# Scan stage: the sum into the states as three products of split operands

## The chip, the cores and the metric

The kernel runs on one core of a Trainium2 chip. The metric is the device time of one execution in microseconds. Times of the kernel before are from three runs, and one more execution was recorded by the hardware profiler; rows below come from that one.

## The reference, cut to what matters

Two transformer-like layers over 2048 rows of 512 values: differential attention, a mixture of experts, a Mamba-2 scan, and a feed-forward block with int8 weights. The change lies in the scan. Per head (64 heads of 64 channels, state size 128), the reference computes

```python
x_dt = x * dt[..., None]
Y_diag = einsum('bclhn,bcshn,bhcls,bcshp->bclhp', C_c, B_c, Lmat, x_dt)
decay_states = exp(A_cum[..., -1:] - A_cum)
states = einsum('bclhn,bhcl,bclhp->bchpn', B_c, decay_states, x_dt)
new = prev * exp(d_k)[..., None, None] + s_k          # step by step
Y_off = einsum('bclhn,bchpn,bhcl->bclhp', C_c, prev_states, exp(A_cum))
g = (Y_diag + Y_off + D_param * x) * silu(z)          # then a row norm, then @ W_out.T
```

`states` is the sum into the states: B of a chunk times x, weighted by dt and by its decay to the end of the chunk.

## The kernel before, in words

The stages are `qkv`, `attention`, `attend_out`, `experts`, `scan` and `finish`, one after the other, each with its own five instruction streams, ordered by hand and tied by semaphores. An engine works its stream strictly in order, so whatever stands behind a waiting instruction waits too. The scan takes the span's stretch from about 1650 to 3175 us.

The scan does 128 steps (`STEPS`): 16 chunks of 128 rows times 8 groups of 8 heads (512 channels). Four steps make a batch (`t // QT`): four chunks of one group. The document calls the steps of a batch the first to the fourth (`t % QT` from 0 to 3). There are 32 batches, and 4 of them belong to group 0. While a batch is scanned, the 8 in-projection tiles of the next one are computed, 3, 2, 2 and 1 in its four steps (`SHARE`), and the convolutions of its four x tiles by VectorE, two in the first and two in the second step (`CONVOLVED`).

In step t the engines do this, in the order of their streams:

- TensorE: `turn_x(t+1)` (transposes of x), `outputs(t)` (fp32 products of 128 columns), `states(t)` (the sum into the states, one fp32 product of 512 columns), some in-projection tiles, `project_out(t-1)`, the other tiles.
- ScalarE: `decays(t+1)` (eight Relu, a table load, one Exp), then `gh` (the high part of the gated output, a Copy to fp32r) and its square, then reads of in-projection tiles and the Silu of convolved tiles (`x_silu`).
- VectorE: `weigh_x(t+1)` gives `xdt`, `weigh_c` gives `ce`, `gate(t)` gives `gx`, `next_state(t)`, `weigh_decays(t+1)` gives `M`, `rest(t)` gives `gl` (the low part), the convolutions, `add_out(t-1)`. In the first step both convolutions stand before `add_out`, in the second one before and one behind.
- GpSimd: `sd` (the decayed state), `decay_inputs(t+1)` gives `xdd` (x with its weights), and `ssq` (sum of squares; in group 0 ScalarE writes it and GpSimd has none).

A value "split" into two fp32r parts is a high part (a Copy to fp32r) and a low part (the rest, a subtraction); `product3` multiplies two split operands with three fp32r products. The in- and out-projection already work so.

The fourth step's `turn_x` needs all four `x_silu` of the next batch, and the last of them stands in the third step of ScalarE's stream, behind `gh` and its square (the list `late`).

Of the kernel before, what the change touches and what calls it, by code (L numbers as in the profile page):

```python
# [956 lines left out]
def experts(nc, g, X, xh, xl, lr, w, space, sources, chan_bc, dt_bias, A_log, mv, hist, x2, D):  # L957
# [25 lines left out]
    with ExitStack() as ctx:  # L983
# [9 lines left out]
        z, dA = carve([P, QT, NH]), carve([P, QT, NH])  # L993
        u, sq = (carve([P, QT * NH]) for n in range(2))
        s2 = sb("ex_s2", [P, QT * NH])
# [3 lines left out]
        rest, ea = carve([NH, CHUNK]), carve([NH, CHUNK])  # L999
        Bt, CB = g.later[:, :].rearrange("p (c n) -> p c n", n=P), g.masked[:, 1, :].rearrange("p (c n) -> p c n", n=P)  # L1000
        bias, eA, chan = sb("ex_bias", [P, NH]), sb("ex_eA", [P, NH]), sb("ex_chan", [P, 2, TAPS + 1])
# [16 lines left out]
        upto_sums, asum_made, ea_made, asum_turned = sem("upto_sums"), sem("asum_made"), sem("ea_made"), sem("asum_turned")  # L1018
        bt, bt_read, cb, cb_made = sem("bt"), sem("bt_read"), sem("cb"), sem("cb_made")
        x2_out, xT_out = sem("x2_out"), sem("xT_out")  # L1020
# [27 lines left out]
        with nc.Block() as block:  # L1048

            @block.sync  # L1050
            def _(sp):
# [13 lines left out]
                for s in range(3, SLOTS + 1):  # L1065
                    if 0 <= s - 3 < TT:
                        sp.wait_ge(normed, s - 2)
                        sp.dma_start(x2[cols(s - 3), :], X[:, s - 3, :]).then_inc(x2_out, 16)
                    i = s - 4
                    if 0 <= i < TT and i % QT == QT - 1:  # L1070
                        c = i // QT
                        sp.wait_ge(x_low, i + 1)
                        for n, part in enumerate((xh, xl)):
                            sp.dma_start(D["xT"][n][:, :, chunk(c)], part[:, :, chunk(c)].bitcast(F32)).then_inc(xT_out, 16)
                    c, part = at(s - 1)
                    if part == 2:
                        for made_by, name, src, out in ((asum_made, "acum", asum, asum_out), (ea_made, "expa", ea, ea_out)):
                            sp.wait_ge(made_by, c + 1)
                            for grp in range(GROUPS):
                                sp.dma_start(D[name][grp * TT + QT * c:grp * TT + QT * (c + 1), :].rearrange("c (h l) -> h c l", l=CL),  # L1080
                                             src[grp * GH:(grp + 1) * GH, :].rearrange("h (c l) -> h c l", l=CL)).then_inc(out, 16)
                    if part == 3:
                        sp.wait_ge(sm_copied, c + 1)
                        sp.wait_ge(sm_exped, 2 * c + 2)
                        sp.wait_ge(sm_turned, c + 1)
                        sp.dma_start(D["small"][:, :, QT * c:QT * (c + 1), :, :], sm[:, :, :, :, :]).then_inc(small_out, 16)
                        sp.wait_ge(bc_silu, c + 1)
                        sp.dma_start(D["C"][:, chunk(c)], acc[:, 1, :]).then_inc(c_out, 16)
                        sp.wait_ge(bt_read, c + 1)
                        sp.dma_start(D["B"][:, QT * c:QT * (c + 1), :], Bt).then_inc(b_out, 16)  # L1090
                        sp.wait_ge(cb_made, c + 1)
                        sp.dma_start(D["CB"][:, QT * c:QT * (c + 1), :], CB).then_inc(cb_out, 16)
                for out, count in ((x2_out, TT), (xT_out, 2 * NCH), (small_out, NCH), (ea_out, GROUPS * NCH), (asum_out, GROUPS * NCH),
                                   (c_out, NCH), (b_out, NCH), (cb_out, NCH)):
                    sp.wait_ge(out, 16 * count)
# [123 lines left out]
            def _(act):  # L1219
# [22 lines left out]
                def scan_part(c, part):  # L1242
# [33 lines left out]
                    if part == 3:  # L1276
                        act.wait_ge(bt, c + 1)
                        if c:
                            act.wait_ge(b_out, 16 * c)
                        act.activation(flat(Bt), bank(c, "bt")[:, :], ACT.Copy).then_inc(bt_read, 1)  # L1280

# [19 lines left out]
            def _(dve):  # L1301
# [66 lines left out]
                def scan_part(c, part):  # L1368
                    if part == 1:
# [3 lines left out]
                        else:  # L1373
# [62 lines left out]
def scan(nc, g, D, tables, hist, ssq_dram, acc_dram, w8, Wgate, Wup):  # L1436
# [26 lines left out]
    with ExitStack() as ctx:  # L1463
# [3 lines left out]
        acc, ssq = sb("sc_acc", [P, QT, E]), sb("sc_ssq", [P, GT, CHUNK])  # L1467
        Bt, Ct, CB = sb("sc_B", [P, QT, NS]), sb("sc_C", [P, CHUNK]), sb("sc_CB", [P, QT, P])
        chan, dtab = sb("sc_chan", [P, DI // P + 2, TAPS + 1]), sb("sc_dtab", [P, DI // P, 2])
# [37 lines left out]
        with nc.Block() as block:  # L1507

            @block.sync
            def _(sp):  # L1510
# [135 lines left out]
            def _(pe):  # L1646
# [74 lines left out]
            def _(act):  # L1721
# [39 lines left out]
                decays(0)  # L1761
                late = []
# [32 lines left out]
            def _(dve):  # L1795
# [483 lines left out]
def two_layers(nc, x, xT, Wq, Wk, Wv, Wo, lq1, lk1, lq2, lk2, first, gate, up, down, lora_b, scan_first, chan_table,  # L2279
# [5 lines left out]
    with ExitStack() as ctx:  # L2285
# [81 lines left out]
```

## Time and profile before

| | us |
|---|---|
| median of three runs | 3590.73 (3584.45 to 3592.86) |
| profiled execution, its own time | 3585.86 |
| its span | 3583.9 |
| TensorE busy over the span | 3375.8 (94%) |
| VectorE busy | 2675.5 (75%) |
| ScalarE busy | 2118.0 (59%) |
| GpSimd busy | 881.7 (25%) |
| `sc_ps` product (the sum into the states), both halves of 128 | 145.1 |
| `sc_xdd` on GpSimd, 128 | 245.9 |

Busy counts the time in which an engine had an instruction under way, a blocked one too. The shares are over the whole span; the scan's own stand in the rows below. The profiled execution is 4.87 us below the median of the three runs.

### The profile page before, as it was taken

How to read it: one execution, taken by the hardware profiler on the slowest of the kernel's cores; microseconds unless marked ns; L12 is line 12 of the kernel's file. 1: busy time of each engine (PE TensorE's matmuls, PEld its weight loads, DVE VectorE, ACT ScalarE, POOL GpSimd, SP SyncE). 2: the span in 40 equal slices, each digit the busy share in tenths (PEclk: the TensorE clock that was granted, in tenths of full speed). 3: DMA queues.
4: the chain of work that ended last, by engine and by line, in shares of the span. 5: the costliest groups of instructions: out<-in, count | busy, mean ns of one | idle time of the engine just before them, and what ended most of it. 6: DMA issues, size and time to landing. Idle time of an engine off the chain costs nothing. (4 is left out here: it accounts for less than half of the span.)

```text
span 3583.9 us, 58360 instructions
## 1 busy us (share of the span) xinstructions
PE 3375.8 (94%) x20672; PEld 2381.6 (66%) x20672; DVE 2675.5 (75%) x5242; ACT 2118.0 (59%) x3392; POOL 881.7 (25%) x818
## 2 busy tenths in 40 slices
PE   8889999999999888986999999999999999979998
PEld 6644444444444466764777777777777777758886
DVE  3577777777777284565999999989999899964444
ACT  3146666666666633443777777777777777753332
POOL 0022222222222210001344434344444344420000
PEclk9989999999999988997999999999999999989999
DMA  7443443443442311137666776677667766640100
GB/s 230 76 89 88 107 99 90 107 90 92 111 83 89 110 39 32 71 103 237 210 223 230 259 237 224 233 245 246 222 221 247 252 227 227 221 144 27 36 12 24
DMA packets 264128, 529.34 MB, mean 148 GB/s; under 512 B 32544, under 2 KB 55200, under 8 KB 260768
## 3 DMA queue, kind: packets, MB, share of 16 engines
q1 hardware_dynamic: 263840, 525.62, 47.2%
q8 instruction: 166, 2.72, 0.3%
q14 instruction: 122, 1.00, 0.1%
HBM read 429.55 MB, written 95.42 MB: 146 GB/s over the span
## 5 line engine op out<-in xcount | busy, mean ns | idle before, releaser
L510 ACT ACTIVATE probs<-prob_scores 128x1024 f32<-128x1024 f32 (+3 forms) x640 | 572.8, 897 | 380.7 <-PE prob_scores L440 372.1
L460 PE MATMUL times_v<-probs,VS 128*64 128x256 f32 (+2 forms) x4608 | 612.4, 382 | 14.1 <-ACT outT L537 13.0
L557 DVE TENSOR_REDUCE part_max<-ring 128x1 f32<-128x512 f32 x720 | 462.7, 685 | 115.5 <-PE ring L432 113.7
L49 PE MATMUL sc_pip<-sc_xh,sc_wl 128*128 128x512 f32 x1024 | 455.0, 444 | 25.0 <-DMA sc_xl<-x_low 18.3
L1618 POOL TENSOR_TENSOR sc_xdd<-sc_xdt,sc_small 128x512 f32<-128x512 f32 x128 | 245.9, 1921 | 844.4 <-DVE sc_xdt L1827 844.4
L460 PEld LDWEIGHTS times_v<-probs,VS 128*64 128x64 f32 x4608 | 279.7, 136 | 253.9 <-issue 162.8
L51 PE MATMUL sc_pip<-sc_xh,sc_wh 128*128 128x512 f32 x1024 | 405.1, 396 | 0.0
L50 PE MATMUL sc_pip<-sc_xl,sc_wh 128*128 128x512 f32 x1024 | 403.8, 394 | 0.0
L1752 ACT ACTIVATE sc_M<-sc_later,sc_small 128x128 f32<-128x128 f32 x1024 | 311.8, 389 | 0.0
L1818 DVE SCALAR_TENSOR_TENSOR sc_ca<-sc_xr,sc_chan,sc_ca 128x512 f32<-128x512 f32 x384 | 290.9, 757 | 13.6
L440 PE MATMUL prob_scores<-QS,KS 50*128 50x512 f32 (+3 forms) x1280 | 298.7, 463 | 1.4 <-ACT probs L510 1.4
L440 PEld LDWEIGHTS prob_scores<-QS,KS 50*128 50x128 f32 x1280 | 119.6, 184 | 214.1 <-ACT probs L510 120.8
L49 PEld LDWEIGHTS sc_pip<-sc_xh,sc_wl 128*128 128x128 f32 x1024 | 193.8, 189 | 100.8 <-issue 44.9
L554 DVE CUSTOM_DVE_ANT_0 masked_scores<-ring,later_keys 128x128 f32<-128x128 f32 x480 | 216.3, 488 | 52.6 <-PE ring L432 49.3
L432 PE MATMUL ring<-KS,QS 48*128 48x512 f32 (+3 forms) x1200 | 235.7, 388 | 12.8 <-DVE part_max L557 8.6
L50 PEld LDWEIGHTS sc_pip<-sc_xl,sc_wh 128*128 128x128 f32 x1024 | 194.1, 190 | 68.0 <-issue 29.2
L1636 POOL TENSOR_TENSOR sc_ssq<-sc_ssq,sc_sq 128x512 f32<-128x512 f32 x112 | 163.4, 1459 | 306.3 <-ACT sc_sq L1780 306.3
L51 PEld LDWEIGHTS sc_pip<-sc_xh,sc_wh 128*128 128x128 f32 x1024 | 193.5, 189 | 43.5
L1667 PE MATMUL sc_py<-sc_M,sc_xdt 128*64 128x128 f32 x2048 | 207.2, 281 | 10.4 <-DVE sc_M L1838 10.4
L368 POOL TENSOR_SCALAR_AFFINE_SELECT probs<-probs 128x256 f32<-128x256 f32 x256 | 104.6, 408 | 456.3 <-ACT probs L510 456.3
L1864 DVE TENSOR_TENSOR sc_gl<-sc_gx,sc_gh 128x512 fp32r<-128x512 f32 x128 | 216.3, 1690 | 0.1
L375 POOL TENSOR_TENSOR w_lo<-w_raw,w_hi 128x512 fp32r<-128x512 f32 x96 | 122.8, 1279 | 354.3 <-ACT w_hi L521 349.0
(328 smaller groups left out, 7179.2 us busy)
## 6 DMA issues: line engine op xcount, KB each, us to landing
sc_wh<-scan_W_high SPq DMA_DIRECT2D x256, 256.0 KB, 2.8
sc_wl<-scan_W_low SPq DMA_DIRECT2D x256, 256.0 KB, 3.5
sc_later<-scan_acum SPq DMA_DIRECT2D x128, 512.0 KB, 4.7
sc_ce<-scan_expa SPq DMA_DIRECT2D x128, 512.0 KB, 5.3
sc_woh<-scan_Wo_high SPq DMA_DIRECT2D x128, 256.0 KB, 4.1
sc_wol<-scan_Wo_low SPq DMA_DIRECT2D x128, 256.0 KB, 4.9
w_raw<-in_Wg SPq DMA_DIRECT2D x64, 256.0 KB, 2.8
scan_W_high<-w_hi SPq DMA_DIRECT2D x64, 256.0 KB, 2.0
```

The source lines that it names most:

```text
L49: pe.matmul(out, ll, rh, start=start, stop=False)
L50: pe.matmul(out, lh, rl, start=False, stop=False)
L51: return pe.matmul(out, lh, rh, start=False, stop=stop)
L432: pe.matmul(slot(place["max", q, t, s])[:, 0:w], QS[q % NQK][rows, i * P:(i + 1) * P], KS[q % NQK][rows, c * CHUNK:c * CHUNK + w], start=T ...
L440: mm = pe.matmul(pb[u % 2][:, s, 0:w], KS[b][rows, j * P:(j + 1) * P], QS[b][rows, (c + 1) * CHUNK - w:(c + 1) * CHUNK], start=True, stop= ...
L460: mm = pe.matmul(po[MV * s:MV * (s + 1), CHUNK - w + n * h:CHUNK - w + (n + 1) * h], VS[p % 2][:, j, :], PT[u % NPT][:, s, n * h:(n + 1) * ...
L510: act.activation(PT[u % NPT][:, :, 0:w], pb[u % 2][:, :, 0:w], ACT.Exp).then_inc(exped, 1)
L554: dve.tensor_tensor_reduce(out=masked_out[:, s, 0:w], in0=slot(n)[:, 0:w], in1=later[:, CHUNK - w:], scale=1.0, scalar=NEG, op0=ALU.add, o ...
L557: dve.tensor_reduce(to, slot(n)[:, 0:w], AX.X, ALU.max).then_inc(emptied, 1)
L1618: pool.tensor_tensor(xdd[t % 2][:, :, :], xdt[t % 2][:, :, :], bc(t, 1), ALU.mult).then_inc(xdd_made, 1)
L1752: act.activation(M[t % 2][:, h, :], later[t % 2][:, h, :], ACT.Relu, bias=small[b % 2][:, c, 3, h:h + 1], scale=-1.0).then_inc(relued, 1)
L1818: dve.scalar_tensor_tensor(out=to, in0=src, scalar=w, in1=to, op0=ALU.mult, op1=ALU.add).then_inc(conv if last else conv_step, 1)
```

## The change

The one fp32 product of `states(t)` becomes `product3` over split operands, B (`Bh`, `Bl`) and the weighted x (`xdh`, `xdl`). B is split once, in the stage `experts`: ScalarE writes the high part where it copied B before, VectorE subtracts the low part, both go to DRAM and the scan loads both. The weighted x is split in each step: GpSimd computes `xdd` as before, but into one buffer instead of two, ScalarE copies it to fp32r (`high_inputs`), GpSimd subtracts (`low_inputs`).

```diff
@@ experts
-        Bt, CB = g.later[:, :].rearrange("p (c n) -> p c n", n=P), ...
+        Bh, Bl = g.later[:, :].bitcast(F32R), usq[:, :].bitcast(F32R)
...
-                        act.activation(flat(Bt), bank(c, "bt")[:, :], ACT.Copy).then_inc(bt_read, 1)
+                        act.activation(Bh[:, :], bank(c, "bt")[:, :], ACT.Copy).then_inc(b_high, 1)
...
+                        dve.wait_ge(b_high, c + 1)
+                        dve.tensor_tensor(Bl[:, :], bank(c, "bt")[:, :], Bh[:, :].bitcast(F32), ALU.subtract).then_inc(bt_read, 1)
@@ scan, SyncE
-                    sp.dma_start(Bt[:, c, :], D["B"][:, at, :]).then_inc(bc_in[c], 16)
+                    for n, part in enumerate((Bh, Bl)):
+                        sp.dma_start(part[:, c, :].bitcast(F32), D["B"][n][:, at, :]).then_inc(bc_in[c], 16)
@@ scan, GpSimd
                 def decay_inputs(t):
                     pool.wait_ge(xdt_made, t + 1)
-                    if t >= 2:
-                        pool.wait_ge(s_prod, t - 1)
-                    pool.tensor_tensor(xdd[t % 2][:, :, :], xdt[t % 2][:, :, :], bc(t, 1), ALU.mult).then_inc(xdd_made, 1)
+                    if t:
+                        pool.wait_ge(xdd_low, t)
+                    pool.tensor_tensor(heads(xdd[:, :]), xdt[t % 2][:, :, :], bc(t, 1), ALU.mult).then_inc(xdd_made, 1)
+
+                def low_inputs(t):
+                    pool.wait_ge(xdd_high, t + 1)
+                    if t:
+                        pool.wait_ge(s_prod, t)
+                    pool.tensor_tensor(xdl[:, :], xdd[:, :], xdh[:, :].bitcast(F32), ALU.subtract).then_inc(xdd_low, 1)
...
                     if t + 1 < STEPS:
                         decay_inputs(t + 1)
+                    if t + 1 < STEPS:
+                        low_inputs(t + 1)
@@ scan, TensorE
                 def states(t):
-                    pe.wait_ge(xdd_made, t + 1)
-                    pe.wait_ge(bc_in[t % QT], 48 * (t // QT // GROUPS + 1))
-                    pe.matmul(p_s[:, :], Bt[:, t % QT, :], xdd[t % 2][:, :, :], start=True, stop=True).then_inc(s_prod, 1)
+                    pe.wait_ge(xdd_low, t + 1)
+                    pe.wait_ge(bc_in[t % QT], 64 * (t // QT // GROUPS + 1))
+                    if t:
+                        pe.wait_ge(s_next, t)
+                    product3(pe, p_s[:, :], (Bh[:, t % QT, :], Bl[:, t % QT, :]), (xdh[:, :], xdl[:, :])).then_inc(s_prod, 1)
@@ scan, ScalarE
+                def high_inputs(t):
+                    act.wait_ge(xdd_made, t + 1)
+                    if t:
+                        act.wait_ge(s_prod, t)
+                    act.activation(xdh[:, :], xdd[:, :], ACT.Copy).then_inc(xdd_high, 1)
...
                     if t + 1 < STEPS:
                         decays(t + 1)
+                        high_inputs(t + 1)
```

On GpSimd, in a step of the last group, before (`sc_sd` begins a step; the three small `sc_ssq` rows stand in that group alone):

```order
L1629 TENSOR_TENSOR sc_sd<-sc_state,sc_small 128x512
L1618 TENSOR_TENSOR sc_xdd<-sc_xdt,sc_small 128x512
L1636 TENSOR_TENSOR sc_ssq<-sc_ssq,sc_sq 128x4x128
L1643 TENSOR_TENSOR sc_ssq<-sc_ssq 128x128 x3
L1629 TENSOR_TENSOR sc_sd<-sc_state,sc_small 128x512
```

and of the change, the same place:

```order
L1648 TENSOR_TENSOR sc_sd<-sc_state,sc_small 128x512
L1630 TENSOR_TENSOR sc_xdd<-sc_xdt,sc_small 128x512
L1636 TENSOR_TENSOR sc_xdl<-sc_xdd,sc_xdh 128x512
L1657 TENSOR_TENSOR sc_ssq<-sc_ssq,sc_sq 128x4x128
L1664 TENSOR_TENSOR sc_ssq<-sc_ssq 128x128 x3
L1648 TENSOR_TENSOR sc_sd<-sc_state,sc_small 128x512
```

One more subtraction stands between `sc_xdd` and `sc_ssq`, so `sc_ssq` and the next step's `sc_sd` are behind it.

On ScalarE, in a second step, before (`sc_M` is the Relu and Exp of `decays`, `sc_pip` an in-projection tile):

```order
L1752 ACTIVATE sc_M<-sc_later,sc_small 128x128 x8
L1755 ACT_TABLE_LOAD
L1755 ACTIVATE sc_M<-sc_M 128x1024
L1772 ACTIVATE sc_gh<-sc_gx 128x512
L1780 ACTIVATE sc_sq<-sc_gx 128x512
L1729 ACTIVATE sc_xr<-sc_pip 128x512
```

and of the change:

```order
L1775 ACTIVATE sc_M<-sc_later,sc_small 128x128 x8
L1778 ACT_TABLE_LOAD
L1778 ACTIVATE sc_M<-sc_M 128x1024
L1788 ACTIVATE sc_xdh<-sc_xdd 128x512
L1803 ACTIVATE sc_gh<-sc_gx 128x512
L1811 ACTIVATE sc_sq<-sc_gx 128x512
L1752 ACTIVATE sc_xr<-sc_pip 128x512
```

The row `sc_xdh` is new and stands behind the Exp and ahead of `sc_gh`; no table load is added. The other rows are those of before.

## Rows read from the trace of the kernel before

**Rows 1.** Busy time by stretch: the scan, then one batch of four steps.

```profile
1686.00:3174.00 1488.00, 1476.31 (x9318) 1165.11 (x9317) 1370.18 (x2110) 1100.40 (x2009) 613.36 (x409) 1.00 0.69 231
...
2499.50:2546.30 46.80, 46.80 (x298) 37.08 (x296) 43.87 (x69) 35.09 (x65) 19.46 (x12) 1.00 0.67 228
```

**Rows 2.** Timeline of TensorE, start of a fourth step: start us, us, engine.

```profile
2521.98 0.40 PE L51 MATMUL sc_pip<-sc_xh,sc_wh 128*128 128x512 f32 x1
2522.21 0.60 PE L1653 MATMUL sc_pxt<-ident,sc_xT 128*128 128x128 f32 x4
...
2524.64 1.13 PE L1677 MATMUL sc_ps<-sc_xdd,sc_B 128*128 128x512 f32 x2
2525.20 0.79 PE L49 MATMUL sc_pip<-sc_xh,sc_wl 128*128 128x512 f32 x1
2525.83 0.39 PE L50 MATMUL sc_pip<-sc_xl,sc_wh 128*128 128x512 f32 x1
```

**Rows 3.** Timeline of GpSimd in a second step.

```profile
2500.44 1.95 POOL L1618 TENSOR_TENSOR sc_xdd<-sc_xdt,sc_small 128x512 f32<-128x512 f32 x1 [7.41 <-DVE sc_xdt L1827]
...
2505.89 1.29 POOL L1636 TENSOR_TENSOR sc_ssq<-sc_ssq,sc_sq 128x512 f32<-128x512 f32 x1 [3.50 <-ACT sc_sq L1780]
2507.14 1.49 POOL L1629 TENSOR_TENSOR sc_sd<-sc_state,sc_small 128x512 f32<-128x512 f32 x1
```

**Rows 4.** Timeline of VectorE in the same second step.

```profile
2500.28 1.21 DVE L1833 TENSOR_TENSOR sc_ce<-sc_ce,sc_C 128x1024 f32<-128x1024 f32 x1
...
2503.17 0.68 DVE L1844 TENSOR_TENSOR sc_state<-sc_sd,sc_ps 128x512 f32<-128x512 f32 x1
2504.80 1.23 DVE L1838 TENSOR_TENSOR sc_M<-sc_M,sc_CB 128x1024 f32<-128x1024 f32 x1 [0.96 <-ACT sc_M L1755]
2505.95 1.78 DVE L1864 TENSOR_TENSOR sc_gl<-sc_gx,sc_gh 128x512 fp32r<-128x512 f32 x1
2507.65 1.00 DVE L1804 COPY sc_xr<-conv_history 128x3 f32<-128x3 f32 x1
...
2508.77 0.54 DVE L1814 TENSOR_SCALAR sc_ca<-sc_xr,sc_chan 128x512 f32<-128x512 f32 x1
```

**Rows 5.** Timeline of ScalarE in the same second step.

```profile
2503.71 1.06 ACT L1755 ACTIVATE sc_M<-sc_M 128x1024 f32<-128x1024 f32 x1
2504.68 0.62 ACT L1772 ACTIVATE sc_gh<-sc_gx 128x512 fp32r<-128x512 f32 x1
2505.20 0.62 ACT L1780 ACTIVATE sc_sq<-sc_gx 128x512 f32<-128x512 f32 x1
```

**Rows 6.** Two source lines: durations in ns, min/median/max.

```profile
L375 POOL TENSOR_TENSOR w_lo<-w_raw,w_hi x96: 1269/1279/1289, 222.1 to 1227.3; 128x512 fp32r<-128x512 f32 x96
...
L1864 DVE TENSOR_TENSOR sc_gl<-sc_gx,sc_gh x128: 678/1783/1796, 1688.9 to 3174.2; 128x512 fp32r<-128x512 f32 x128
```

**Rows 7.** Timeline of VectorE around the next first step.

```profile
2531.35 0.69 DVE L1875 TENSOR_TENSOR sc_acc<-sc_acc,sc_pop 128x512 f32<-128x512 f32 x1 [0.67 <-PE sc_pop L51]
...
2532.55 1.22 DVE L1833 TENSOR_TENSOR sc_ce<-sc_ce,sc_C 128x1024 f32<-128x1024 f32 x1
...
2536.06 1.22 DVE L1838 TENSOR_TENSOR sc_M<-sc_M,sc_CB 128x1024 f32<-128x1024 f32 x1
...
2538.91 1.00 DVE L1804 COPY sc_xr<-conv_history 128x3 f32<-128x3 f32 x1
```

**Rows 8.** Timeline of ScalarE, then GpSimd, in the same stretch.

```profile
2534.31 1.06 ACT L1755 ACTIVATE sc_M<-sc_M 128x1024 f32<-128x1024 f32 x1
...
2530.09 1.50 POOL L1629 TENSOR_TENSOR sc_sd<-sc_state,sc_small 128x512 f32<-128x512 f32 x1
```

**Rows 9.** Timeline of ScalarE in the third step between them.

```profile
2518.88 0.63 ACT L1772 ACTIVATE sc_gh<-sc_gx 128x512 fp32r<-128x512 f32 x1 [1.83 <-DVE sc_gx L1858]
...
2521.35 0.64 ACT L1742 ACTIVATE sc_xT<-sc_ca 128x512 f32<-128x512 f32 x1
```

**Rows 10.** Timeline of VectorE, fourth step of a batch of group 0.

```profile
2476.06 0.69 DVE L1827 TENSOR_TENSOR sc_xdt<-sc_pxt,sc_small 128x512 f32<-128x512 f32 x1 [2.21 <-issue]
```

More of the change, by code:

```diff
@@ L993, in experts @@
         z, dA = carve([P, QT, NH]), carve([P, QT, NH])
-        u, sq = (carve([P, QT * NH]) for n in range(2))
+        usq = carve([P, CHUNK])
+        u, sq = usq[:, 0:QT * NH], usq[:, QT * NH:]
         s2 = sb("ex_s2", [P, QT * NH])
@@ L999, in experts @@
         rest, ea = carve([NH, CHUNK]), carve([NH, CHUNK])
-        Bt, CB = g.later[:, :].rearrange("p (c n) -> p c n", n=P), g.masked[:, 1, :].rearrange("p (c n) -> p c n", n=P)
+        Bh, Bl = g.later[:, :].bitcast(F32R), usq[:, :].bitcast(F32R)
+        CB = g.masked[:, 1, :].rearrange("p (c n) -> p c n", n=P)
         bias, eA, chan = sb("ex_bias", [P, NH]), sb("ex_eA", [P, NH]), sb("ex_chan", [P, 2, TAPS + 1])
@@ L1018, in experts @@
         upto_sums, asum_made, ea_made, asum_turned = sem("upto_sums"), sem("asum_made"), sem("ea_made"), sem("asum_turned")
-        bt, bt_read, cb, cb_made = sem("bt"), sem("bt_read"), sem("cb"), sem("cb_made")
+        bt, b_high, bt_read, cb, cb_made = sem("bt"), sem("b_high"), sem("bt_read"), sem("cb"), sem("cb_made")
         x2_out, xT_out = sem("x2_out"), sem("xT_out")
@@ L1089, in _ @@
                         sp.wait_ge(bt_read, c + 1)
-                        sp.dma_start(D["B"][:, QT * c:QT * (c + 1), :], Bt).then_inc(b_out, 16)
+                        for n, part in enumerate((Bh, Bl)):
+                            sp.dma_start(D["B"][n][:, QT * c:QT * (c + 1), :], part[:, :].bitcast(F32).rearrange("p (c n) -> p c n", n=P)).then_inc(b_out, 16)
                         sp.wait_ge(cb_made, c + 1)
@@ L1093, in _ @@
                 for out, count in ((x2_out, TT), (xT_out, 2 * NCH), (small_out, NCH), (ea_out, GROUPS * NCH), (asum_out, GROUPS * NCH),
-                                   (c_out, NCH), (b_out, NCH), (cb_out, NCH)):
+                                   (c_out, NCH), (b_out, 2 * NCH), (cb_out, NCH)):
                     sp.wait_ge(out, 16 * count)
@@ L1378, in scan_part @@
                         dve.wait_ge(z_biased, c + 1)
+                        if c:
+                            dve.wait_ge(b_out, 32 * c)
                         dve.scalar_tensor_tensor(out=u[:, :], in0=zf, scalar=-1.0, in1=zf, op0=ALU.mult, op1=ALU.max).then_inc(u_made, 1)
@@ L1467, in scan @@
         acc, ssq = sb("sc_acc", [P, QT, E]), sb("sc_ssq", [P, GT, CHUNK])
-        Bt, Ct, CB = sb("sc_B", [P, QT, NS]), sb("sc_C", [P, CHUNK]), sb("sc_CB", [P, QT, P])
+        Bh, Bl = sb("sc_Bh", [P, QT, NS], F32R), sb("sc_Bl", [P, QT, NS], F32R)
+        Ct, CB = sb("sc_C", [P, CHUNK]), sb("sc_CB", [P, QT, P])
         chan, dtab = sb("sc_chan", [P, DI // P + 2, TAPS + 1]), sb("sc_dtab", [P, DI // P, 2])
@@ L1480, in scan @@
         xdt = [sb(f"sc_xdt{b}", [P, GH, HP]) for b in range(2)]
-        xdd = [sb(f"sc_xdd{b}", [P, GH, HP]) for b in range(2)]
+        xdd, xdh, xdl = sb("sc_xdd", [P, GC]), sb("sc_xdh", [P, GC], F32R), sb("sc_xdl", [P, GC], F32R)
         st, sd = sb("sc_state", [P, GROUPS, GC]), sb("sc_sd", [P, GC])
@@ L1497, in scan @@
         relued, exped, decay, xt, xdt_made, xdd_made, ce_made = (sem(n) for n in ("relued", "exped", "decay", "xt", "xdt_made", "xdd_made", "ce_made"))
+        xdd_high, xdd_low = sem("xdd_high"), sem("xdd_low")
         y_prod, s_prod, s_decayed, s_next = sem("y_prod"), sem("s_prod"), sem("s_decayed"), sem("s_next")
@@ L1521, in load_bc @@
                     c, at = t % QT, chunk_of(t)
-                    sp.dma_start(Bt[:, c, :], D["B"][:, at, :]).then_inc(bc_in[c], 16)
+                    for n, part in enumerate((Bh, Bl)):
+                        sp.dma_start(part[:, c, :].bitcast(F32), D["B"][n][:, at, :]).then_inc(bc_in[c], 16)
                     sp.dma_start(Ct[:, c * CL:(c + 1) * CL], D["C"][:, at * CL:(at + 1) * CL]).then_inc(bc_in[c], 16)
@@ L1760, in _ @@
                         x_silu(n - 1)
+                def high_inputs(t):
[3 more added lines that the diff above has]
+                    act.activation(xdh[:, :], xdd[:, :], ACT.Copy).then_inc(xdd_high, 1)
                 decays(0)
+                high_inputs(0)
                 late = []
@@ L1831, in weigh_c @@
                     dve.wait_ge(e_in[t % NE], 16 * (t // NE + 1))
-                    dve.wait_ge(bc_in[c], 48 * (t // QT // GROUPS + 1))
+                    dve.wait_ge(bc_in[c], 64 * (t // QT // GROUPS + 1))
                     dve.tensor_tensor(ce[t % NE][:, :, :], ce[t % NE][:, :, :],
@@ L2289, in two_layers @@
         D = dict(small=dram("scan_small", [P, GROUPS, TT, KINDS, GH]), acum=dram("scan_acum", [GROUPS * TT, GH * CL]),
-                 B=dram("scan_B", [P, TT, NS]), C=dram("scan_C", [P, T]), CB=dram("scan_CB", [P, TT, P]),
+                 B=[dram(f"scan_B_{s}", [P, TT, NS]) for s in ("high", "low")], C=dram("scan_C", [P, T]), CB=dram("scan_CB", [P, TT, P]),
                  expa=dram("scan_expa", [GROUPS * TT, GH * CL]),
```

3 lines of the change are left out of this document (2 added, 1 removed).

## Prediction

> **What bounds the kernel now.** I began with the busy times by stretch. In the scan TensorE is busy 1476.31 of 1488 us at full clock, VectorE 1370.18, ScalarE 1100.40, GpSimd 613.36 [rows 1]. So TensorE sets the pace, but VectorE is close behind; whether its spare time is usable has to be read from the order of the work. A batch of four steps is a period of 46.8 us in which TensorE has no gap and VectorE is busy 43.87 [rows 1].
>
> Then I read the timelines of one batch, engine by engine, to find where the engines wait for each other. One loop through all of them comes out. VectorE's `add_out` in the fourth step waits 0.67 us for TensorE's `project_out` and starts at 2531.35 [rows 7]. From there VectorE works through the first and second steps, with two convolutions each, practically without a stop. The last Silu of the next batch's x then runs on ScalarE behind `gh` of the third step, from 2521.35 to 2521.99 in the batch before [rows 9], and TensorE's `turn_x` starts at 2522.21 [rows 2]. So that loop (VectorE in two long steps, ScalarE's late Silu, TensorE from `turn_x` to the end of `project_out`) is as long as TensorE's own work, but for 2522.21 - 2521.99 = 0.22 us. That is all the slack there is in a batch. What lengthens VectorE's first two steps by more than this stops TensorE.
>
> **The change part by part.**
>
> *TensorE.* The fp32 product starts at 2524.64, the next fp32r product at 2525.20 and the one behind that at 2525.83 [rows 2]; fp32r products follow each other by 0.23 us (2521.98 to 2522.21, [rows 2]). From 2524.64 to 2525.83 are 1.19 us for the fp32 product and one fp32r product, so the fp32 one costs 1.19 - 0.23 = 0.96 us. Three fp32r products cost 0.69. The saving is 0.27 us a step. Its lower bound is about 0.05 us, if the join between fp32 and fp32r work (the first fp32r product behind the fp32 one takes 0.63 until the next starts) keeps some 0.2 us of its own; its upper bound is 0.27. I take 0.27, since one join stands before and after the change. Over 128 steps this is 35 us, if TensorE were alone.
>
> *ScalarE.* One Copy to fp32r of 128x512 a step, 0.62 us by `gh` [rows 5], some 0.55 in a chain. No table load comes with it (the order of the change shows none). It stands ahead of `gh`. In the first step its input is there in time. In the second, Exp ends at 2504.77 and `gh` starts at 2504.68 by the record [rows 5], so `gh` slips to about 2505.2 and ends at 2505.8, still before VectorE is through with `M` at 2506.03 [rows 4]. So the Copy itself costs nothing; that cover is `M`, and without it 0.55 us a step would be due.
>
> *GpSimd.* One subtraction a step of two 128x512 operands into fp32r. The nearest row is the same form in the stage of attention: 1279 ns with hardly any spread [rows 6]. GpSimd has the time, 613 of 1488 us. But VectorE pays for it. VectorE's `gl` takes 678 ns at best and 1783 in the median [rows 6]. In the second step it starts at 2505.95, with GpSimd's `ssq` under way from 2505.89 to 2507.18, and ends at 2507.73 [rows 3, 4]: it stood still for 1.1 us. The small copy behind it, of 3 columns, takes 1.00 us and ends at 2508.65, just when GpSimd's `sd` (2507.14 to 2508.63) is done [rows 3, 4]. The other way round, `xdd` takes 1.95 us, from 2500.44 to 2502.39 [rows 3], because it starts during VectorE's `ce`, which ends at 2501.49 [rows 4]. The two engines exclude each other for whole instructions, unless VectorE reads one operand from PSUM (`gx`, beside `xdd`, is of that kind), and the one that has waited goes first.
>
> The Trainium skill says it so in "SBUF — State Buffer", section "Who interferes with whom": VectorE with two SBUF inputs and GpSimd take turns at a shared port pair, and the later one blocks fully. By that alone every added subtraction could stop VectorE for 1.28 us, four times a batch, 5.1 us; laid out in the rows, as below, the first two steps pay 2.7.
>
> Where does `xdl` fall? It needs ScalarE's Copy, which ends 0.55 us after Exp.
>
> Second step: Copy done at 2505.3, inside VectorE's `M` (2504.80 to 2506.03, [rows 4]). The state add starts at 2503.17 and VectorE idles 0.96 us ahead of `M` [rows 4], but that lies before the Copy and gives no cover. `xdl` waits for `M`, runs to 2507.2, and `gl` waits for it just as it did for `ssq`. But `ssq` comes now behind it: it waits for `gl` (to 2507.8), runs to 2509.0 and holds up the small copy, and `sd` runs from 2509.05 to 2510.1 and holds up the first pass of the convolution, which starts at 2510.2 instead of 2508.77 [rows 4]. Cost 1.4 us.
>
> First step: in the fourth step before it `ssq` moves back likewise, to 2532.0, and `sd`, which ran from 2530.09 [rows 8], to 2533.1, so that `ce` ends 0.5 us later than its 2533.77 [rows 7]. The Exp ends at 2535.37 [rows 8], Copy at 2535.95, `xdl` runs from 2536.0 to 2537.3, and `M`, which started at 2536.06 [rows 7], starts when that is over, 1.2 us later. `ssq` and `sd` stand behind it in the same way as before, the small copy of 2538.91 ends at about 2541.2 instead of 2539.91 [rows 7]. Cost 1.3 us, the 0.5 of `ce` within it.
>
> Third step: `xdl` falls on the state add, which is free, and then on `M`, 0.65 us; but that is behind `gx`, so not in the loop. The fourth step has its waits on Exp and on TensorE to absorb it.
>
> *The rest.* Two B loads instead of one in a new chunk, four subtractions and four DMAs in `experts`: a few us at most, beside TensorE's work there; I count 0. The single buffer of `xdd` makes GpSimd wait for its own last subtraction, which is always done.
>
> *Sum.* Per batch: 1.4 + 1.3 for VectorE, less 0.22 slack, less 0.27 that the one `states` in the loop saves: 2.2 us. In group 0 GpSimd has no `ssq`, and the fourth step's `xdt` waits 2.21 us for TensorE [rows 10], which swallows it: there 0. So 28 x 2.2 = 62 us. On the profiled execution's 3585.86 us that is 3648; the median of the runs lies 4.87 above it, so 3652.
>
> The bounds of the unknown cost, GpSimd's subtraction in its place: if only one of the two places costs, 1.3 - 0.49 = 0.8 a batch, 23 us, 3614. If each is as dear as GpSimd's `xdd` with its waits, 1.95 [rows 3], and so 0.67 dearer than 1.28, 2.2 + 1.3 = 3.5 a batch, 98 us, 3689.
>
> **The rivals.**
>
> *The saving comes home (faster).* VectorE loses nothing in the loop, if GpSimd's subtraction gives way instead of going first, or fits beside operands from PSUM (`gx`, state add, `xdt`, `add_out`). It decides below 0.22 us of added stop a batch. For it: TensorE is the engine without gaps, and VectorE is only 92% busy. Against it: the idle ahead of `M` lies before the Copy can start, and `gl`'s median in [rows 6] is the stopped one. Time: 35 us less, 3556; with the lower bound of the saving, 6 us less, 3585. Chance 0.14.
>
> *A draw.* Half of one place costs, as much as slack and saving (0.49 a batch) give: 3584 to 3598. Chance 0.07.
>
> *TensorE waits for the split itself.* `states` now needs `xdd`, Copy and `xdl` in a row. In the fourth step `states` starts at 2524.64 [rows 2], and its `xdl`, made in the third, is over by about 2520. Some 4 us are spare, so it comes only if GpSimd's queue falls behind; it would cost 1 us or more a step, 128 us, 3720. Chance 0.04.
>
> **How the numbers follow.** A measurement of this kernel tells 0.2% from no change, 7 us. The forecast, VectorE's loop, gets 0.75, with its own range 3614 to 3689; I widen to 3600 to 3695 to take in the edge of the draw and some of TensorE's waiting. That leaves out the faster rival and most of the two small ones. Slower: 0.75 + 0.04 = 0.79. Within 0.2%: 0.07. Faster: 0.14.
>
> **What would show it.** In the scan TensorE's gaps should grow from 12 us to some 70, nearly all ahead of `turn_x` in fourth steps, ended by ScalarE's Silu. VectorE's small copies and first convolution passes should be longer, its busy time up by 80 us or more; `xdl` at 1.3 us alone and near 2 behind `M`; `states` at 0.69. A batch should take 49 us. If TensorE has no gaps and a batch takes 45.7, the faster rival holds; if its gaps stand ahead of `sc_ps`, the third.

## The result, and the profile after

The changed kernel took 3653.55 us (median of 4 runs, 3650.24 to 3657.31), the kernel before 3589.88 us beside it. The ratio is 1.0179 (95% interval 1.0165 to 1.0193): slower by 64 us, where 3652 had been forecast. The profiled execution took 3650.24, with a span of 3648.3.

The total agrees better than its parts. Cut at fixed events of the two traces (VectorE's first `sc_xdt`, its last `sc_gl`, the last read of `ex_px`, the first `sc_pip` matmul), the time went as follows. Each stretch runs from the start of one of these instructions to the start of the next:

| stretch | before, us | after, us | difference | forecast |
|---|---|---|---|---|
| end of `experts` (last `ex_px` read to first `sc_pip`) | 39.7 | 50.0 | +10.3 | 0 |
| first `sc_pip` to first `sc_xdt` | 35.4 | 37.1 | +1.7 | 0 |
| the scan's steps (first `sc_xdt` to last `sc_gl`) | 1498.9 | 1551.0 | +52.1 | +62 |
| behind the scan | 409.7 | 409.6 | -0.1 | 0 |

Start with the page of the kernel after, busy time by engine. VectorE is busy 2767.5 us and GpSimd 1118.2.

```profile
PE 3375.7 (93%) x20800; PEld 2414.4 (66%) x20800; DVE 2767.5 (76%) x5246; ACT 2185.4 (60%) x3520; POOL 1118.2 (31%) x946
```

Busy time by stretch, with the columns of [rows 1]: the scan first, then three batches in a row.

```profile
1686.00:3238.00 1552.00, 1483.41 (x9492) 1203.90 (x9492) 1463.70 (x2116) 1177.85 (x2158) 855.09 (x540) 0.99 0.66 224
...
2563.00:2612.00 49.00, 46.76 (x302) 37.83 (x300) 46.86 (x69) 37.39 (x69) 26.73 (x17) 1.00 0.64 217
2612.00:2662.60 50.60, 48.19 (x300) 39.33 (x300) 47.86 (x69) 38.56 (x70) 28.05 (x18) 0.97 0.61 210
2662.60:2710.30 47.70, 46.56 (x300) 37.86 (x300) 45.62 (x69) 36.13 (x68) 25.52 (x16) 1.00 0.65 223
```

TensorE, which had no gap in the batch of [rows 1], now idles 2.24 us in the first of these, and its gaps in the scan grew from 12 to 69 us. VectorE is busy 93.5 us more in the scan. The three batches are 49.0, 50.6 and 47.7 us, by `sc_gl` to `sc_gl` 48.8, 50.6 and 47.7, and so it goes on in threes. Their mean is 49.0, where 49 had been forecast. Nearly all of the added waiting of TensorE, 53 of 57 us, stands where it was looked for. The waits of TensorE in the scan (engine, tile, line, what it waited for: us in total, times, longest):

```profile
PE sc_pxt L1674 <- ACT sc_xT L1765: 53.1, 31, 2.3
```

That is `turn_x` in fourth steps, ended by ScalarE's late Silu, 31 times. There is no row for `sc_ps`, so `states` never waited for the split.

Now one second step, against [rows 3, 4]: VectorE's timeline, then GpSimd's.

```profile
2546.99 1.22 DVE L1869 TENSOR_TENSOR sc_M<-sc_M,sc_CB 128x1024 f32<-128x1024 f32 x1 [0.73 <-ACT sc_M L1778]
2548.13 1.79 DVE L1895 TENSOR_TENSOR sc_gl<-sc_gx,sc_gh 128x512 fp32r<-128x512 f32 x1
2549.85 1.26 DVE L1835 COPY sc_xr<-conv_history 128x3 f32<-128x3 f32 x1
2551.14 0.97 DVE L1839 COPY conv_history<-sc_xr 128x3 f32<-128x3 f32 x1
2552.02 0.54 DVE L1845 TENSOR_SCALAR sc_ca<-sc_xr,sc_chan 128x512 f32<-128x512 f32 x1
...
2547.56 1.82 POOL L1636 TENSOR_TENSOR sc_xdl<-sc_xdd,sc_xdh 128x512 fp32r<-128x512 f32 x1 [2.75 <-ACT sc_xdh L1788]
2549.34 1.74 POOL L1657 TENSOR_TENSOR sc_ssq<-sc_ssq,sc_sq 128x512 f32<-128x512 f32 x1
2551.04 1.04 POOL L1648 TENSOR_TENSOR sc_sd<-sc_state,sc_small 128x512 f32<-128x512 f32 x1
```

The order is the one forecast: `xdl` is asked for inside `M` and runs when `M` is over, `gl` waits for it, the first small copy waits for `ssq`. Only at the end it differs: `sd` falls on the second small copy (0.97 us for 3 columns), not on the first pass of the convolution. From the start of `M` to the first pass are 2552.02 - 2546.99 = 5.03 us, against 2508.77 - 2504.80 = 3.97 before [rows 4]: 1.06 us more. In front of it the wait for Exp fell from 0.96 to 0.73, since ScalarE has read its in-projection tile earlier there and comes to Exp 0.23 us sooner, counted from `sc_xdt`.

A stop costs VectorE 0.8 to 1.1 us: `gl` takes 1.79 instead of 0.68, the first copy of 3 columns 1.26 instead of 0.16, the second one 0.97 instead of 0.17. No `gl` is free any more. The two source lines, durations in ns as min/median/max, against [rows 6]:

```profile
L1895 DVE TENSOR_TENSOR sc_gl<-sc_gx,sc_gh x128: 1484/1780/1797, 1701.3 to 3238.7; 128x512 fp32r<-128x512 f32 x128
...
L1636 POOL TENSOR_TENSOR sc_xdl<-sc_xdd,sc_xdh x128: 1288/1811/2367, 1693.1 to 3231.7; 128x512 fp32r<-128x512 f32 x128
```

The end of a fourth step on TensorE, against [rows 2], with the three new products:

```profile
2505.85 0.39 PE L1691 MATMUL sc_py<-sc_ce,sc_state 128*64 128x128 f32 x4
2506.17 0.50 PE L49 MATMUL sc_ps<-sc_xdh,sc_Bl 128*128 128x512 f32 x1
2506.51 0.40 PE L50 MATMUL sc_ps<-sc_xdl,sc_Bh 128*128 128x512 f32 x1
2506.74 0.40 PE L51 MATMUL sc_ps<-sc_xdh,sc_Bh 128*128 128x512 f32 x1
2506.97 0.40 PE L49 MATMUL sc_pip<-sc_xh,sc_wl 128*128 128x512 f32 x1
```

They start 0.34, 0.23 and 0.23 us apart: 0.80 in all, not 0.69. The join with the fp32 work stands now ahead of the first of them and keeps 0.11 us.

The 10.3 us of `experts` are a wait that the forecast counted as nothing. VectorE's waits there, first row, and the DMA queue ahead of it:

```profile
DVE A L1385 <- DMA scan_B_low<-A: 8.8, 2, 7.8
...
1607.15 2.62 SPq L1083 DMA_DIRECT2D scan_acum<-ex_asum  x5
1609.82 2.71 SPq L1083 DMA_DIRECT2D scan_expa<-A  x8
...
1615.03 0.77 SPq L1094 DMA_DIRECT2D scan_B_low<-A  x1
```

The low part of B shares its space with `u`. So for the last chunk `u` waits until the third chunk's `scan_B_low` has left, and SP comes to it only at 1615.03, behind the small DMAs. `u` starts at 1618.34 instead of 1608.99, and TensorE (`ex_misc`, L1185) waits for what follows it.

### The profile page after: what moved, and what is told of

Read it like the earlier page. It is cut to its first block and busy times, and to the rows that moved or that the text cites. A ratio compares the mean times of both kernels' runs of the same rounds, so it can differ in the third digit from the quotient of the medians.

```text
span 3648.3 us, 59154 instructions
## 1 busy us (share of the span) xinstructions
PE 3375.7 (93%) x20800; PEld 2414.4 (66%) x20800; DVE 2767.5 (76%) x5246; ACT 2185.4 (60%) x3520; POOL 1118.2 (31%) x946
## 3 DMA queue, kind: packets, MB, share of 16 engines
q14 instruction: 126, 1.03, 0.1%
## 5 line engine op out<-in xcount | busy, mean ns | idle before, releaser
L49 PE MATMUL sc_pip<-sc_xh,sc_wl 128*128 128x512 f32 x1024 | 408.9, 399 | 27.0 <-DMA sc_xl<-x_low 19.0
L1636 POOL TENSOR_TENSOR sc_xdl<-sc_xdd,sc_xdh 128x512 fp32r<-128x512 f32 x128 | 213.6, 1669 | 226.1 <-ACT sc_xdh L1788 226.1
L1895 DVE TENSOR_TENSOR sc_gl<-sc_gx,sc_gh 128x512 fp32r<-128x512 f32 x128 | 224.7, 1756 | 0.7
```

The source lines that it names most:

```text
L49: pe.matmul(out, ll, rh, start=start, stop=False)
L1895: dve.tensor_tensor(gl[t % 2][:, :, :], gx[:, :, :], gh[t % 2][:, :, :].bitcast(F32), ALU.subtract).then_inc(g_low, 1)
```

## The experiments

Runs of one chip share the kernel before: 3592.19 us (3587.52 to 3595.73, 13 runs) for e1 to e4, 3588.43 (3583.09 to 3594.69, 13 runs) for e5 to e7. "Scan" below is the stretch of the table, first `sc_xdt` to last `sc_gl`; the stretches of before the scan vary by some us from one execution to another.

### e1: `u` in a space of its own

```
-        usq = carve([P, CHUNK])
-        u, sq = usq[:, 0:QT * NH], usq[:, QT * NH:]
+        u, sq = sb("ex_u", [P, QT * NH])[:, :], dA[:, :, :].rearrange("p c h -> p (c h)")
...
-                        if c:
-                            dve.wait_ge(b_out, 32 * c)
```

> In the trace of the changed kernel VectorE stops 7.84 us in the experts stage, where it may write u of the last chunk only after the low part of B of the chunk before has left the shared space. Here u and sq lie elsewhere (u in a space of its own, sq over dA), and the wait is gone; the scan is untouched. Theory, that this wait sits on the path: the scan begins about 11 us earlier and the time falls from 3653.6 to 3643. Rival, that the late start has another cause (the extra DMAs of B, the subtraction behind the high part): 3650 or more, with the scan beginning at most 3 us earlier.

Measured: 3648.34 us (3642.57 to 3649.15), ratio 1.0151 (1.0134 to 1.0168), against 1.0179 (1.0165 to 1.0193) with the shared space. The two intervals touch, and 3648 lies between the theory's 3643 and the rival's 3650, so the total alone does not decide. The trace does: the end of `experts` is 40.1 us again. The scan is 1554.7 here, 3.7 more than in the changed kernel: most of that is one slow batch more, the first (50.2 us instead of 47.7), of the kind told below under the clock. VectorE's `u` of the last chunk, first in the kernel after, then in e1:

```profile
1618.34 0.43 DVE L1385 SCALAR_TENSOR_TENSOR A<-A 128x256 f32<-128x256 f32 x1 [7.84 <-DMA scan_B_low<-A]
```

```profile
1614.32 0.43 DVE L1383 SCALAR_TENSOR_TENSOR ex_u<-A 128x256 f32<-128x256 f32 x1
```

Counted from the last read of `ex_px` (1600.6 and 1605.5), `u` comes 17.8 us later in the one and 8.8 in the other. The wait on the low part of B was worth 10 us, and it has nothing to do with the products.

### e2: no GpSimd subtraction

The low part of the weighted x is left out; the second product reads the high part in its place. Copy and three products remain.

```
-                    if t + 1 < STEPS:
-                        low_inputs(t + 1)
...
-                    product3(pe, p_s[:, :], (Bh[:, t % QT, :], Bl[:, t % QT, :]), (xdh[:, :], xdl[:, :])).then_inc(s_prod, 1)
+                    product3(pe, p_s[:, :], (Bh[:, t % QT, :], Bl[:, t % QT, :]), (xdh[:, :], xdh[:, :])).then_inc(s_prod, 1)
```

> The changed kernel without GpSimd's subtraction; the low part of the weighted x is left out, and the product that should read it reads the high part, so TensorE and ScalarE do the same work as in the changed kernel. The experts stage keeps its 11 us. Theory, VectorE's loop stopped by GpSimd's subtraction: without it the loop is 46.58 - 0.27 = 46.3 us a batch against 46.8 before, so 16 us less than before and 11 more for the experts stage, 3585. Were TensorE alone the bound once the subtraction is gone, 35 less and 11 more, 3566. Rival, that the chain from the weighted x over ScalarE's Copy to the product is what costs: 3640 or more.

Measured: 3585.99 us, ratio 0.9982 (0.9973 to 0.9991). The scan is 1483.1, 15.8 less than before, although e2 still has the 10 us in `experts` (its end takes 50.9). There is no wait at `turn_x` left. An ordinary batch is 46.5 us. So the subtraction carries the whole loss of the scan. It also gives the true saving of TensorE, which now sets the pace alone: a batch before is 46.87 us from `sc_gl` to `sc_gl`, and 46.87 - 46.5 is some 0.4 us a batch, 0.1 a step.

### e3: the kernel before, with an idle GpSimd subtraction

A subtraction of `xdd` from itself into a space that nobody reads, behind Exp, once a step. Nothing is left out.

```
+                        pool.wait_ge(exped, t + 2)
+                        pool.wait_ge(xdd_made, t + 2)
...
+                        pool.tensor_tensor(idle[:, :, :], xdd[(t + 1) % 2][:, :, :], xdd[(t + 1) % 2][:, :, :], ALU.subtract).then_inc(more, 1)
```

> The kernel before, with one added GpSimd subtraction of 128x512 in each step, behind the weighted x and after Exp, whose result nobody reads: nothing waits for it but GpSimd's own next work. Theory, that VectorE and GpSimd exclude each other: 1.4 + 1.3 - 0.22 = 2.5 us a batch of the 28 with sums of squares, up to 69 us, or about 60 if scaled to what the changed kernel's scan lost; 3650 to 3660. Rival, that only the chain and the three products cost: 3590, as before.

Measured: 3635.76 us (3634.4 to 3638.28), ratio 1.0122 (1.0107 to 1.0137). The scan grew by 45.6 us, and TensorE waits 39.6 us for the late Silu, 31 times. The direction is the theory's, the size under its range. The second step shows the same picture as the changed kernel; timelines of VectorE and GpSimd in e3:

```profile
2586.63 1.23 DVE L1845 TENSOR_TENSOR sc_M<-sc_M,sc_CB 128x1024 f32<-128x1024 f32 x1 [0.73 <-ACT sc_M L1762]
2587.77 1.53 DVE L1871 TENSOR_TENSOR sc_gl<-sc_gx,sc_gh 128x512 fp32r<-128x512 f32 x1
2589.23 1.25 DVE L1811 COPY sc_xr<-conv_history 128x3 f32<-128x3 f32 x1
2590.51 0.97 DVE L1815 COPY conv_history<-sc_xr 128x3 f32<-128x3 f32 x1
...
2586.68 2.08 POOL L1638 TENSOR_TENSOR sc_idle<-sc_xdd 128x512 fp32r<-128x512 f32 x1 [2.23 <-ACT sc_M L1762]
```

In the first step the idle operation does not wait for a Copy. It runs at 2570.36 beside the state add (1.04 us long, not stopped), and `M` behind it takes 1.57 instead of 1.22: 0.35 us there instead of 1.1. That is why e3 is cheaper than was expected.

### e4: the subtraction on VectorE, behind `M`

```
+                    dve.tensor_tensor(xdl[:, :], xdd[:, :], xdh[:, :].bitcast(F32), ALU.subtract).then_inc(xdd_low, 1)
```

> The changed kernel with the subtraction done by VectorE behind the weighing of the decays, GpSimd's work as before. Theory: VectorE pays 0.69 us in each of the first two steps instead of 1.3 and 1.4, so 1.38 - 0.49 = 0.9 us a batch, 25 us, with the experts stage's 11 about 3626. Rival, that a step pays for the chain or for VectorE's total load (its busy time rises by 88 us instead of standing still): 3650 or more.

Measured: 3649.69 us (3646.64 to 3653.24), ratio 1.016 (1.0145 to 1.0175): a miss by over 20 us. The scan is 1546.3, 47.4 more than before. VectorE's timeline in e4, a third step:

```profile
2613.29 1.22 DVE L1860 TENSOR_TENSOR sc_M<-sc_M,sc_CB 128x1024 f32<-128x1024 f32 x1
2614.43 1.75 DVE L1867 TENSOR_TENSOR sc_xdl<-sc_xdd,sc_xdh 128x512 fp32r<-128x512 f32 x1
2616.10 1.53 DVE L1892 TENSOR_TENSOR sc_gl<-sc_gx,sc_gh 128x512 fp32r<-128x512 f32 x1
```

VectorE's own subtraction takes its 0.69 us at best, but here it is the one that `ssq` stops, and `gl` behind it is stopped by `sd`. In a first step it is the same, but there the small copy has become free. I had counted the first two steps, and they cost less than counted (0.57 and 0.38 us more than before); I had left out the third. A third step now takes 8.95 us instead of 7.63, and there is no wait for TensorE at `add_out` any more (1.8 us, 4 times, in the scan) that could take it in. A batch is one unbroken run of VectorE of 49.1 us, with only the wait for Exp in it. The expectation's rival, VectorE's total load, holds here, and GpSimd was not the culprit by itself: a full-width operation more costs VectorE about as much on either engine.

### e5: e1, and the Copy ahead of Exp in second steps

```
+                    if between is not None:
+                        between(t)
                     act.wait_ge(relued, GH * (t + 1))
...
+                        if c == 1:
+                            decays(t + 1, high_inputs)
```

> The kernel after with u of experts in its own space (as e1), and in the second step of each batch ScalarE's Copy of the weighted x stands between the Relus and the Exp, so that GpSimd's subtraction can run in the time in which VectorE is idle ahead of M (0.73 us there after the change, 0.96 before). Nothing is left out. Theory (VectorE pays for each GpSimd instruction that falls beside its work): the second step cost 1.06 us for the subtraction; up to that comes back, less the 0.55 us by which Exp slips, where M waits for it. Net 0.3 to 0.85 us a batch, 32 batches: 10 to 27 us less than e1's 3648, so 3621 to 3638. Rival (the Exp that slips costs as much as the subtraction's place gives): 3645 to 3652. If the place of the subtraction were of no matter at all and only the late Exp counted: 0.55 x 32 = 18 us more, 3666.

Measured: 3632.95 us (3628.07 to 3636.75), ratio 1.0124 (1.0109 to 1.0139), where e1 has 1.0151 (1.0134 to 1.0168); the intervals touch, so the reading rests on the rows below. The scan is 1543.3, 11.3 less than in e1, at the low end of the 10 to 27 us that were expected. A second step in e5, VectorE and then GpSimd:

```profile
2681.30 0.68 DVE L1878 TENSOR_TENSOR sc_state<-sc_sd,sc_ps 128x512 f32<-128x512 f32 x1
2683.60 1.22 DVE L1872 TENSOR_TENSOR sc_M<-sc_M,sc_CB 128x1024 f32<-128x1024 f32 x1 [1.62 <-ACT sc_M L1778]
2684.75 1.79 DVE L1898 TENSOR_TENSOR sc_gl<-sc_gx,sc_gh 128x512 fp32r<-128x512 f32 x1
2686.46 1.00 DVE L1838 COPY sc_xr<-conv_history 128x3 f32<-128x3 f32 x1
...
2681.28 1.29 POOL L1634 TENSOR_TENSOR sc_xdl<-sc_xdd,sc_xdh 128x512 fp32r<-128x512 f32 x1 [0.74 <-ACT sc_xdh L1788]
2684.69 1.30 POOL L1655 TENSOR_TENSOR sc_ssq<-sc_ssq,sc_sq 128x512 f32<-128x512 f32 x1 [2.12 <-ACT sc_sq L1814]
```

`xdl` runs beside the state add and in VectorE's idle time, takes 1.29 us and stops nothing: the state add keeps its 0.68. One of the three stops is gone, 1.06 us. But `M` waits 1.62 us for Exp instead of 0.73, 0.65 for the Copy and 0.24 in which the Copy itself waits for `xdd`. The net is 0.17 us a batch, some 5 us. The other half of the gain over e1 stands in single batches, at the start of the scan above all, and is not explained by this.

### e6: two products, with no Copy and no subtraction

On top of e1. GpSimd writes the weighted x as fp32r. The low part of the weighted x is left out of the states.

```
-                    pool.tensor_tensor(heads(xdd[:, :]), xdt[t % 2][:, :, :], bc(t, 1), ALU.mult).then_inc(xdd_made, 1)
+                    pool.tensor_tensor(heads(xdh[t % 2][:, :]), xdt[t % 2][:, :, :], bc(t, 1), ALU.mult).then_inc(xdd_made, 1)
...
+                    pe.matmul(p_s[:, :], Bl[:, t % QT, :], xdh[t % 2][:, :], start=True, stop=False)
+                    pe.matmul(p_s[:, :], Bh[:, t % QT, :], xdh[t % 2][:, :], start=False, stop=True).then_inc(s_prod, 1)
```

> The kernel after with u in its own space, and with GpSimd writing the weighted x straight to fp32r (two buffers), so that there is no Copy, no subtraction and two products instead of three: the low part of the weighted x is left out of the states. TensorE has 0.96 - 0.46 = 0.50 us less a step than before the change by the rows (0.35 to 0.4 if the join between fp32 and fp32r work remains). If TensorE alone set the time, 128 steps would give 45 to 64 us: 3526 to 3545. Theory (the loop through VectorE's first two steps, ScalarE's late Silu and TensorE's turn_x to project_out, in which only one of the four products of a batch stands, plus 0.22 us of slack that is no gain but shows as TensorE's gap): 0.4 to 0.5 a batch, 32 batches, 13 to 16 us less than before's 3592: about 3577, and TensorE has gaps ahead of turn_x in fourth steps of some 1.5 us a batch.

Measured: 3562.03 us (3557.81 to 3567.24), ratio 0.9927 (0.9908 to 0.9945). This is the fastest of all, 26 us under the kernel before, at the price of the low part. A fourth step's start on TensorE:

```profile
2601.91 0.39 PE L51 MATMUL sc_pip<-sc_xh,sc_wh 128*128 128x512 f32 x1
2602.88 0.66 PE L1663 MATMUL sc_pxt<-ident,sc_xT 128*128 128x128 f32 x4 [0.58 <-ACT sc_xT L1755]
```

The gaps ahead of `turn_x` are there, as the loop would have it, but 0.6 us a batch instead of 1.5, since a product less saves less than I took from the rows of before. An ordinary batch is 46.1 us. The gain went past the loop theory's 3577 and short of TensorE's 3526 to 3545. The loop sets the pace again, and TensorE stands by 14.4 us in all. It went past 3577 because VectorE's second step is also shorter than before, 15.37 us instead of 15.61: as in the changed kernel, `M` waits 0.72 us for Exp and not 0.96. Against e2, with its 46.5, one product less is worth 0.4 us a batch; had TensorE alone set the pace, it would be four times 0.23.

### e7: e1 without GpSimd's addition of the squares

The sums of squares of groups 1 to 7 are left out. Copy, subtraction and three products are all there.

```
-                        pool.tensor_tensor(ssq[:, :, at], ssq[:, :, at], sq[:, :, :], ALU.add).then_inc(sq_add, 1)
```

> The kernel after with u in its own space and without GpSimd's addition of the squares in each step (the sums of squares of groups 1 to 7 are left out); Copy, subtraction and three products are all there. GpSimd then has about as much to do in a step as before the change. Theory (what costs is one more GpSimd instruction beside VectorE, whichever it is): the scan falls by as much as it had grown and some more, since TensorE's saving then comes in: 1483 to 1500 us instead of e1's 1554.6, total 3577 to 3594. Rival (the chain of Copy, subtraction and states itself costs, or ScalarE's Copy does): the scan stays at 1540 to 1555, total 3635 to 3648.

Measured: 3580.57 us (3576.69 to 3588.83), ratio 0.9977 (0.9968 to 0.9987). The scan is 1488.5, against 1554.7 in e1. TensorE's wait at `turn_x` in e7:

```profile
PE sc_pxt L1668 <- ACT sc_xT L1759: 3.6, 6, 2.0
```

Another GpSimd instruction of the same length was taken away, and the whole loss of the scan went with it; a batch is 46.5 us as in e2. The chain of Copy, subtraction and `states` is innocent. What counts is how many GpSimd instructions fall beside VectorE's `M`, `gl` and small copies, and by e4 the same operation in VectorE's own stream is no cheaper.

## Why the prediction held, point by point

**The loop.** It was right. TensorE's gaps went from 12 to 69 us (some 70 forecast) and stand at `turn_x` in fourth steps, behind ScalarE's Silu. An ordinary batch is 49.0 us on average, as forecast. e2, e3 and e7 show that GpSimd's count of instructions makes it so.

**The second step, 1.4 us.** The stops in it cost 1.06, and the wait for Exp ahead of `M` gave back 0.23, so the step grew by 0.84 (VectorE, `sc_xdt` to `sc_xdt`: 15.60 to 16.44). I had taken GpSimd's length, 1.28 us, as VectorE's loss, and pushed `sd` onto the convolution. What VectorE loses is 1.1 us for a stop by `xdl` or `ssq` and 0.8 for one by `sd`, and `sd` fell on the second small copy.

**The first step, 1.3 us.** It grew from 14.58 to 15.92 in two batches of three, 1.34 us, with 0.30 of it in `ce` (1.51 to 1.56 instead of 1.22) where I had 0.5. In the third, behind the slow products told below, it takes 15.10. The order differs from the forecast. `M` did not wait for `xdl`. Since VectorE comes later into this step, Exp is done before `M` is asked for, `M` goes first and `xdl` is stopped, as the next rows show: VectorE's `ce` in an ordinary first step, then the rest from the first step behind group 0, where `ce` is not stopped but the order is the same: VectorE, ScalarE's Exp and Copy, GpSimd.

```profile
2575.57 1.51 DVE L1864 TENSOR_TENSOR sc_ce<-sc_ce,sc_C 128x1024 f32<-128x1024 f32 x1
...
2530.55 1.22 DVE L1869 TENSOR_TENSOR sc_M<-sc_M,sc_CB 128x1024 f32<-128x1024 f32 x1
2531.70 1.79 DVE L1895 TENSOR_TENSOR sc_gl<-sc_gx,sc_gh 128x512 fp32r<-128x512 f32 x1
2533.41 1.25 DVE L1835 COPY sc_xr<-conv_history 128x3 f32<-128x3 f32 x1
...
2529.46 1.06 ACT L1778 ACTIVATE sc_M<-sc_M 128x1024 f32<-128x1024 f32 x1
2530.43 0.61 ACT L1788 ACTIVATE sc_xdh<-sc_xdd 128x512 fp32r<-128x512 f32 x1
...
2531.11 1.82 POOL L1636 TENSOR_TENSOR sc_xdl<-sc_xdd,sc_xdh 128x512 fp32r<-128x512 f32 x1 [1.99 <-ACT sc_xdh L1788]
```

The price is that of the second step all the same: three stops instead of two.

**Third and fourth steps.** 0.65 us was forecast for the third, off the loop. It grew by 0.41 (7.63 to 8.04) and the fourth shrank by 0.65 (9.05 to 8.40), as its waits took it in; in every third batch the slow products told below lengthen it to some 10.

**TensorE's saving, 0.27 us a step.** This term was mis-sized. e2 and e7, where TensorE is without gaps again, give 46.87 - 46.5 = 0.4 us a batch, 0.1 a step. The rows at the place give 0.16: 1.19 us for the fp32 product and one fp32r product before, 0.80 + 0.23 = 1.03 after. Where the other 0.06 goes is open. "One join stands before and after the change" was right, but its price had been booked to the fp32 product alone. The lower bound of 0.05 was nearer.

**The sum.** VectorE's four steps make the ordinary batch 1.34 + 0.84 + 0.41 - 0.65 = 1.94 longer, 48.8 us. In the prediction's own form it is 1.34 + 0.84, less 0.22 slack and less the 0.1 to 0.16 that one `states` saves: 1.80 to 1.86, where 2.2 had been forecast. Every third batch adds something that was not in the forecast, told below, and the mean of three is +2.17, beside the forecast's 2.2. "28 x" was too much. The difference is 2.17 us in 18 ordinary batches, six in a row between two of group 0 (39 us), 1.6 on average in the six that follow in the last four chunks (48.3 us in most, 9.5 us together), and some 4 us in all the others, around group 0. Together some 52 us, not 62.

**The rest, "I count 0".** This step failed, and it is the one whose mechanism was missed. It had looked at the work that was added in `experts` and not at the buffer that was shared: the wait `b_out` ahead of `u` puts VectorE behind SP's queue. It measured 10.3 us, and e1 removes it. So the total is right partly by luck: 10 us too much in the scan met 10 us too little in `experts`, and within the scan some 5 us of slow products, which I had not forecast, made up for stops that cost less than was said.

**The rivals.** The saving came home nowhere, since no `gl` ran free. `states` did not wait: `xdl` is done 4.5 us ahead of it in fourth steps and 3.2 at the least in an ordinary batch.

## What to carry to other kernels

Before GpSimd gets one more operation in a loop that VectorE nearly fills, count the stops at the places where both have work, and price each by what the stopped instruction loses: here even a copy of 3 columns paid the full 1.1 us. To move the operation to VectorE is no way out when VectorE's own steps are part of the loop (e4). In these traces a GpSimd operation was free in a gap of VectorE, or beside an instruction with an operand from PSUM; check that its input is there by then. When two buffers are folded into one, look for who writes the space next and for the slowest reader of what is in it, which may be a DMA behind others in its queue.

## What the hardware showed that was not expected

**The clock.** In every third ordinary batch TensorE's products behind the wait for the Silu are slow. TensorE's timeline of such a fourth step in the kernel after, and the start of another one without slow products; then the granted clock (third column from the right) in stretches of 4 us around the slow one, around the batch before it, and around the other one:

```profile
2611.41 0.39 PE L51 MATMUL sc_pip<-sc_xh,sc_wh 128*128 128x512 f32 x1
2614.08 0.66 PE L1674 MATMUL sc_pxt<-ident,sc_xT 128*128 128x128 f32 x4 [2.27 <-ACT sc_xT L1765]
...
2617.99 0.69 PE L49 MATMUL sc_ps<-sc_xdh,sc_Bl 128*128 128x512 f32 x1
...
2319.68 0.66 PE L1674 MATMUL sc_pxt<-ident,sc_xT 128*128 128x128 f32 x4 [2.28 <-ACT sc_xT L1765]
```

```profile
2614.00:2618.00 4.00, 3.92 (x37) 3.43 (x37) 3.16 (x4) 3.98 (x12) 3.62 (x3) 0.63 0.48 186
...
2565.00:2569.00 4.00, 3.72 (x41) 3.19 (x42) 4.00 (x7) 3.98 (x12) 3.62 (x3) 1.00 0.71 229
...
2319.00:2323.00 4.00, 3.32 (x40) 2.86 (x41) 4.00 (x6) 3.98 (x12) 3.62 (x3) 1.00 0.61 239
```

From the start of `sc_py` to that of `sc_ps` are 3.32 us (2614.67 to 2617.99), against 1.90 in the batch before (2565.87 to 2567.77). The granted clock is 0.63 over the stretch and 1.00 in the other, so TensorE ran part of it at 1.2 GHz, the lower of its two levels. (In the Trainium skill, "TensorE: Matmul & The Clock Gate", section "What's actually happening", TensorE falls to 1.2 GHz when it has been idle; the rows agree that it does behind a gap.) The length of the gap does not decide it alone: behind one of 2.28 us, at 2319.68, the clock stayed at 1.00, and behind one of 1.75 us, ahead of the `turn_x` at 3149.87, it fell. A slow batch takes 50.6 us instead of 48.8, and the next one, 47.7, gets most of it back, since its first step takes 15.10 us instead of 15.92: there `ce` is not stopped, `xdl` starts beside the state add and holds `M` up by 0.5 us only, and just one small copy is stopped. Over three that leaves 0.7 us, and there are seven such batches, so about 5 us of the scan. This is read from the traces alone; e1 and e5 have such batches too (50.6 and 50.4 us). No run tested it. In e3, where TensorE waits 1.4 to 1.5 us at this place in ordinary batches, these all take 48.5 or 48.6 us.

**Who goes next.** Where VectorE and GpSimd both have work, they took turns instruction by instruction: `M`, `xdl`, `gl`, `ssq`, copy, `sd`, copy. In these rows neither does two in a row while the other is waiting, though VectorE's queue is full. The small copies of 3 columns take part in this and wait 0.8 to 1.1 us for their turn.
